# A linear-attention block with a routed feed-forward: the second attention product with swapped operands in four column tiles

## The reference, cut to what matters

```python
q, k, v = heads(x Wq + bq), heads(x Wk + bk), heads(x Wv + bv)     # b h s d
qp = relu(einsum('bhsd,hdf->bhsf', q, rw)) + EPS                   # EPS = 1e-6
kp = relu(einsum('bhsd,hdf->bhsf', k, rw)) + EPS
kv = einsum('bhsf,bhsd->bhfd', kp, v)
qkv = einsum('bhsf,bhfd->bhsd', qp, kv)
norm = einsum('bhsf,bhf->bhs', qp, kp.sum(axis=2))
x = layernorm(x + (qkv / (norm + EPS)) Wo + bo)
x = layernorm(x + ffn(x))     # gated mlp of width 1024, and experts chosen by product keys, 4 heads
```

## Time and profile before

| | |
|---|---|
| time, median of 3 runs | 3632.07 us (3629.95 to 3634.01) |
| profiled execution | 3635.19 us, span 3633.4 us |
| granted TensorE clock | 0.991 of full speed |
| instructions | 52250 |
| DMA | 61.17 MB, mean 17 GB/s |

### The profile page before, as it was taken

The page is one execution under the profiler, slowest core; times in us unless marked ns, Lnnn a source line. Parts: engine busy times, 40 slices in busy tenths (PEclk is TensorE's granted clock), DMA queues, the critical chain, the costliest instruction groups (busy, mean ns, idle before and its releaser), DMA issues.

```text
span 3633.4 us, 52250 instructions
## 1 busy us (share of the span) xinstructions
PE 3549.2 (98%) x19420; PEld 2929.1 (81%) x19420; DVE 2585.7 (71%) x5554; ACT 1981.3 (55%) x2886; POOL 1514.3 (42%) x1012
## 2 busy tenths in 40 slices
PE   8789999999999999999999999999999999999988
PEld 6668888888888888888888888888888888888877
DVE  4577777777777777777777777777677777777773
ACT  4455465555555555556555555555655554555551
POOL 0354344443344434444433444443444434555440
PEclk9899999999999999999999999999999999999999
DMA  3000000000000000000000000000000000000000
GB/s 118 18 12 18 13 13 12 18 18 12 12 18 12 18 18 13 12 18 13 18 18 13 13 13 18 18 14 17 13 12 18 18 7 12 13 13 12 7 6 12
DMA packets 23339, 61.17 MB, mean 17 GB/s; under 512 B 5552, under 2 KB 10032, under 8 KB 23088
## 3 DMA queue, kind: packets, MB, share of 16 engines
q1 hardware_dynamic: 18480, 41.04, 3.6%
q0 software_dynamic: 4608, 16.78, 1.1%
HBM read 41.04 MB, written 16.78 MB: 16 GB/s over the span
## 4 chain that ended last, share of the span: by engine, by line
PE 90%; DVE 3%; ACT 3%; POOL 1%; issue 1%; SPq 0%; DMA 0%; DVEq 0%; ACTq 0%; POOLq 0%
PE ring L639 28%; PE y_bank L732 12%; PE y_bank L734 11%; PE step_bank L554 6%; PE step_bank L562 6%; PE step_bank L666 6%; PE step_bank L639 5%; PE step_bank L598 3%; PE step_bank L656 3%; PE step_bank L548 3%; PE step_bank L590 3%; PE step_bank L712 3%; PE y_bank L728 1%; POOL grid L461 1%; DVE prob L1120 1%
## 5 line engine op out<-in xcount | busy, mean ns | idle before, releaser
L461 POOL TENSOR_TENSOR grid<-ex 128x1024 f32<-128x1024 f32 x512 | 1066.3, 2090 | 999.2 <-DVE prob L1117 364.3
L732 PE MATMUL y_bank<-wd_sb,gate 128*128 128x256 f32 x2048 | 621.6, 385 | 0.0
L734 PE MATMUL y_bank<-up_sb,wexp 128*128 128x256 f32 x2048 | 609.1, 379 | 0.0
L1107 DVE SCALAR_TENSOR_TENSOR grid<-grid,best 128x1024 f32<-128x1024 f32 x256 | 329.0, 1285 | 328.2 <-POOL grid L461 327.3
L1120 DVE SCALAR_TENSOR_TENSOR prob<-grid,narrow,prob 128x1024 f32<-128x1024 f32 x256 | 450.7, 1760 | 7.9
L639 PE MATMUL ring<-x1T_hl,downT_hl 128*128 128x512 f32 x1536 | 421.3, 409 | 17.2 <-ACT gate L883 17.2
L639 PE MATMUL ring<-x1T_hl,wg_hl 128*128 128x512 f32 x1536 | 428.8, 414 | 3.1 <-DVE gate L1136 3.1
L734 PEld LDWEIGHTS y_bank<-up_sb,wexp 128*128 128x128 f32 x2048 | 389.1, 190 | 52.8
L639 PE MATMUL ring<-x1T_hl,wu_hl 128*128 128x512 f32 x1536 | 422.2, 410 | 0.0
L732 PEld LDWEIGHTS y_bank<-wd_sb,gate 128*128 128x128 f32 x2048 | 354.0, 190 | 50.8 <-issue 22.7
L883 ACT ACTIVATE gate<-ring,bg_sb 128x512 f32<-128x512 f32 x256 | 176.3, 689 | 396.7 <-PE ring L639 395.0
(11 more groups left out here) (159 smaller groups left out, 5920.9 us busy)
## 6 DMA issues: line engine op xcount, KB each, us to landing
xb<-in_L_attn_x SPq DMA_DIRECT2D x34, 512.0 KB, 3.7
out_y<-x POOLq DMA_DIRECT2D x32, 512.0 KB, 3.0
xa<-in_L_attn_x SPq DMA_DIRECT2D x30, 512.0 KB, 3.7
prob<-in_L_ffn_down_embed SPq DMA_DIRECT2D x1, 1024.0 KB, 5.8
prob<-in_L_ffn_Wg SPq DMA_DIRECT2D x1, 1024.0 KB, 8.6
prob<-in_L_ffn_Wu SPq DMA_DIRECT2D x1, 1024.0 KB, 10.5
wd_sb<-in_L_ffn_Wd SPq DMA_DIRECT2D x1, 1024.0 KB, 11.4
up_sb<-in_L_ffn_up_embed SPq DMA_DIRECT2D x1, 1024.0 KB, 12.1
```

Source lines behind the costliest of these rows:

```text
L461: pool.tensor_tensor(grid[:, h % 2], bcast(ex[:, h, 0:NX].unsqueeze(2), [P, NX, NK]), bcast(ex[:, RH + h, 0:NK].unsqueeze(1), [P, NX, NK]) ...
L732: pe.matmul(rows, gate[:, c % 2, t * P:(t + 1) * P], wd_sb[:, c, :], start=(c == 0 and t % 2 == 0), stop=False, skip_group_check=True)
L734: mm = pe.matmul(rows, wexp[:, c % 2, t * P:(t + 1) * P], up_sb[:, c, :], start=False, stop=(c == C - 1), skip_group_check=True)
L1107: marks["keep", h] = rt_steps.mark(dve.scalar_tensor_tensor(out=g, in0=g, scalar=best[:, h, TOP - 1:TOP], in1=g, op0=ALU.is_ge, op1=ALU.mult))
```

## The change

The second product swaps its operands. The stationary operand is now 32 columns of `kv_blocks` (two heads by 16), the moving one qp with all 512 rows. Four such matmuls write the partitions 0, 32, 64 and 96 of one bank, so the result is transposed already, 128 of the 256 dimensions per bank. "num" gives the numerators so, and "den" the denominators, each repeated over its head's 16 dimensions, from a second set of blocks. The four "qkv" and two "back" uses become two "den" and two "num". ACT reads den, adding a constant, into `attnT` (now the memory of x1); DVE's new step "divide" takes the reciprocal of 128x512 in place and multiplies it with num plus a constant.

POOL no longer adds EPS to qp; a "consts" use after each fold multiplies the blocks with -0.5 and gives DVE the two constants. v is no longer biased: ACT copies it out of its bank, without bv. What bv adds is bv Wo, computed once into bo, less the EPS share in the constants. wo's sum and the norm's statistics are now in xb, and L1072's counterpart writes x1. xb's next load waits for that one. SP issues the store, in place of POOL. The uses stand at other chunks: den 0 and num 0 early in chunk 3, divide 0 in its middle, den 1 and num 1 early in chunk 5, divide 1 in its middle, wo 0 and wo 1 in chunk 6 as before.

In the tables qkv and back go; den and num get WORK 0.95 each and HOLD 2.0 and 8.0, consts 0.6 and 2.0. DVE's wait for y_stored moves to ACT's den 0; bv is loaded by element with the later weights.

```diff
@@ -59,10 +59,10 @@
               + [("v", 1)] + KV_TILE[2] + KV_TILE[3])
-    AT_SEQ = ([("turn", 0), ("turn", 1), ("q", 0), ("q", 1)] + [("qp", j) for j in range(4)] + [("qkv", 0)]
-              + [("qp", 4), ("qp", 5), ("qkv", 1), ("qp", 6), ("qp", 7), ("qkv", 2), ("qkv", 3)]
-              + [("back", 0), ("back", 1), ("wo", 0), ("wo", 1), ("next", 0), ("next", 1)])
-    KV_USES, AT_USES = len(KV_SEQ), len(AT_SEQ)
+    AT_SEQ = ([[("turn", 0)], [("turn", 1)], [("q", 0)], [("q", 1)]] + [[("qp", j)] for j in range(4)] + [[]]
+              + [[("den", 0), ("num", 0)], [("divide", 0), ("qp", 4)]] + [[("qp", j)] for j in range(5, 8)] + [[]]
+              + [[("den", 1), ("num", 1)], [("divide", 1)], [], [("wo", 0)], [("wo", 1)], []])
+    KV_USES = len(KV_SEQ)
     STEP_BANKS, FILL = 4, BG // 2
@@ -100,15 +101,16 @@
         kv_sum = sb("kv_sum", P, FC // 2 * P)
-        kv_blocks = sb("kv_blocks", P, FC, 2, DK + 1)
+        kv_blocks = sb("kv_blocks", P, 2, FC, 2, DK)
+        num_w, den_w = kv_blocks[:, 0], kv_blocks[:, 1]
...
         xbT = qp[:, 2:4]
-        den = sb("den", P, T, 4)
-        attnT = xbT
+        consts = sb("consts", P, 4)
         x1 = sb("x1", P, T, D)
+        attnT = x1[:].rearrange("p t d -> p (t d)").rearrange("p (h n) -> p h n", h=2)
         stats, mv1, rstd1 = sb("stats", P, T, 6), sb("mv1", P, T, 2), sb("rstd1", P, T)
@@ -177,20 +180,18 @@
-        AT_EARLY = [AT_SEQ[3 * c:3 * c + 1] for c in range(7)] + [[]]
-        AT_MID = [AT_SEQ[3 * c + 1:3 * c + 2] if c < 6 else [] for c in range(7)] + [[]]
-        AT_LATE = [AT_SEQ[3 * c + 2:3 * c + 3] for c in range(6)] + [[], AT_SEQ[-2:]]
-        AT_MID[6] = [("wo", 1)]
+        AT_EARLY, AT_MID, AT_LATE = ([AT_SEQ[3 * c + k] for c in range(C - 1)] for k in range(3))
+        AT_EARLY.append([]), AT_MID.append([]), AT_LATE.append([("next", 0), ("next", 1)])
         kv_places = [(c, place) for c in range(C) for place in range(3) if place or c >= C - 2]
...
-        WORK = {"turn": 0.44, "k": 1.73, "q": 1.73, "v": 1.73, "kp": 0.47, "qp": 0.46, "qkv": 1.73, "sum": 1.73,
-                "back": 0.44, "wo": 1.73, "next": 0.44, "rt": 1.39, "pt": 0.44, "fold": 2.6, "ff": 1.39, "out": 1.73}
-        HOLD = {"turn": 2.0, "k": 6.0, "q": 6.0, "v": 4.0, "kp": 2.0, "qp": 2.0, "qkv": 3.5, "sum": 3.0,
-                "back": 2.0, "wo": 3.0, "next": 5.0, "rt": 8.0, "pt": 5.0, "fold": 9.0}
+        WORK = {"turn": 0.44, "k": 1.73, "q": 1.73, "v": 1.73, "kp": 0.47, "qp": 0.46, "den": 0.95, "num": 0.95, "consts": 0.6, "sum": 1.73,
+                "wo": 1.73, "next": 0.44, "rt": 1.39, "pt": 0.44, "fold": 2.6, "ff": 1.39, "out": 1.73}
+        HOLD = {"turn": 2.0, "k": 6.0, "q": 6.0, "v": 4.0, "kp": 2.0, "qp": 2.0, "den": 2.0, "num": 8.0, "consts": 2.0, "sum": 3.0,
+                "wo": 3.0, "next": 5.0, "rt": 8.0, "pt": 5.0, "fold": 9.0}
         place, taken = {}, [0] * (STEP_BANKS + 2)
@@ -388,10 +390,14 @@
                     else:
-                        sp.wait_ge(*drained("at", m - 1, "wo", 1))
+                        sp.wait_ge(x1_ready, m * T)
                     sp.dma_start(xb[:], x_groups[m]).then_inc(xb_loaded, 16)
+                if last:
+                    sp.wait_ge(y_ready, (f + 1) * T)
+                    sp.dma_start(out_groups[f], y_sb[:]).then_inc(y_stored, 16)
             schedule(sp, body, lambda b: None)
+            sp.wait_ge(y_stored, 16 * NG)
@@ -440,13 +446,10 @@
                     pool.wait_ge(*full("at", m, "turn", 1))
+                    if m == 0:
+                        pool.wait_ge(bo_ready, 2)
                     pool.tensor_tensor(xb[:], xb[:], bcast(bo_sb[:].unsqueeze(1), [P, T, D]),
                                        ALU.add).then_inc(xb_bias, 1)
-
-                def qp_add(j):
-                    wait_apart(pool, drained("at", m, "qp", j))
-                    pool.tensor_scalar(qp[:, j % 4], qp[:, j % 4], ATTN_EPS, 1.0, ALU.add,
-                                       ALU.mult).then_inc(qp_eps, 1)
@@ -603,8 +594,29 @@
             pe.wait_ge(low_ready, 3)
+            for k in range(KD):
+                mm = pe.matmul(ring[0][:, 0:D], bv_sb[:, k:k + 1].broadcast_to([P, P]), wo_sb[:, k, :],
+                               start=(k == 0), stop=(k == KD - 1))
+            mm.then_inc(bo_full, 1)
             for k in (STEP_BANKS, STEP_BANKS + 1):
                 pe.wait_ge(bank_read[k], fill_taken[k])
+
+            def weights(kind, c):
+
+                return (num_w if kind == "num" else den_w)[:, c].rearrange("p g d -> p (g d)")
+
+            def consts_use(a):
+
+                bank = bank_of("kv", a, "consts", 0)
+                free(pe, "kv", a, "consts", 0)
+                pe.wait_ge(blocks_ready, 3 * (a // BG + 1))
+                pe.wait_ge(*drained("kv", a, "fold", 0))
+                for col, kind in enumerate(("num", "den")):
+                    for c in range(FC):
+                        row, at = 2 * DK * (c % 4), 2 * col + c // 4
+                        mm = pe.matmul(bank[row:row + 2 * DK, at:at + 1], weights(kind, c), neg_half[:, 0:1],
+                                       start=True, stop=True)
+                filled_by(mm, "kv", a, "consts", 0)
@@ -655,23 +669,19 @@
                                            qT_hl[:, j // 2, :], start=(part == 0), stop=(part == 1))
-                    elif kind == "qkv":
-                        pe.wait_ge(qp_eps, m * FC + 2 * j + 2)
-                        if j == 0:
-                            pe.wait_ge(blocks_ready, 3 * batch)
-                            pe.wait_ge(*drained("kv", batch * BG - 1, "fold", 0))
-                        W = 2 * (DK + 1)
-                        for t in range(T):
-                            for c in range(2):
-                                mm = pe.matmul(at_bank[:, (2 * t + c) * W:(2 * t + c + 1) * W],
-                                               qp[:, (2 * j + c) % 4, t * P:(t + 1) * P],
-                                               kv_blocks[:, 2 * j + c].rearrange("p a b -> p (a b)"),
-                                               start=True, stop=True)
-                    elif kind == "back":
-                        pe.wait_ge(*drained("at", m, "qkv", 2 * j + 1))
-                        mm = turn(at_bank, x1, j)
+                    elif kind in ("den", "num"):
+                        if kind == "den":
+                            for k in range(4):
+                                pe.wait_ge(*drained("at", m, "qp", 4 * j + k))
+                            if j == 0:
+                                pe.wait_ge(blocks_ready, 3 * batch)
+                                pe.wait_ge(*drained("kv", batch * BG - 1, "fold", 0))
+                        for k in range(4):
+                            mm = pe.matmul(at_bank[2 * DK * k:2 * DK * (k + 1), :], weights(kind, 4 * j + k),
+                                           qp[:, k, :], start=True, stop=True)
                     elif kind == "wo":
-                        pe.wait_ge(*drained("at", m, "back", 1))
+                        pe.wait_ge(*drained("at", m, "num", 0))
+                        pe.wait_ge(*drained("at", m, "num", 1))
                         mm = project_rows(at_bank, attnT, wo_sb, 2 * j)
@@ -848,8 +865,12 @@
                         read_by(act.activation(qp[:, j % 4, :], at_bank[:], ACT.Relu), "at", m, kind, j)
-                    elif kind == "back":
-                        read_by(act.copy(attnT[:, j, :], at_bank[:]), "at", m, kind, j)
+                    elif kind == "den":
+                        if last and j == 0:
+                            act.wait_ge(y_stored, (it - LAST_LAG + 1) * 16)
+                        act.wait_ge(*drained("kv", batch * BG - 1, "consts", 0))
+                        read_by(act.activation(attnT[:, j, :], at_bank[:], ACT.Identity,
+                                               bias=consts[:, 2 + j:3 + j]), "at", m, kind, j)
                     else:
@@ -998,23 +1015,35 @@
+            dve.wait_ge(w_loaded, W_ALL)
+            dve.tensor_scalar(bv_eps[:], bv_sb[:], -ATTN_EPS, None, ALU.mult).then_inc(bo_ready, 1)
+            dve.wait_ge(bo_full, 1)
+            dve.tensor_tensor(bo_sb[:], ring[0][:, 0:D], bo_sb[:], ALU.add).then_inc(bo_ready, 1)
+
             def blocks(b):
...
                 sums = bank[:, 0:FC * VW].rearrange("p (c w) -> p c w", c=FC)
-                bias = bv_sb[:].rearrange("p (c w) -> p c w", c=FC)
                 for g2 in range(2):
                     rows, cols = slice(g2 * F, (g2 + 1) * F), slice(g2 * DK, (g2 + 1) * DK)
-                    dve.scalar_tensor_tensor(out=kv_blocks[rows, :, g2, 0:DK], in0=bias[rows, :, cols],
-                                             scalar=ATTN_EPS * S, in1=sums[rows, :, cols], op0=ALU.mult,
-                                             op1=ALU.add).then_inc(blocks_ready, 1)
-                    ins = dve.tensor_scalar(kv_blocks[rows, :, g2, DK:DK + 1], sums[rows, :, 2 * DK:VW],
```

(40 more changed lines are left out.)

59 lines of the change are left out of this document (29 added, 30 removed).

## The result

The changed kernel takes 3730.83 us (median of 4 runs, 3728.46 to 3733.95) against 3632.39 (3629.95 to 3634.01): a ratio of 1.0272 (95% interval 1.0254 to 1.0290). It is 98 us slower. The forecast was 3553, range 3508 to 3620; it was wrong in sign. Its profiled execution took 3731.7 us against 3635.2 before, span 3729.9 against 3633.4; mean granted clock of TensorE 0.973 against 0.991.

The account below looks back on a forecast made before the run. TensorE, busy 98% of the span, was taken as the bound. 81 us from 26 groups plus 3 from 6 others, less 5 for consts and bv, gave 79: 3556 us profiled, 3553 median, range 3508 to 3620.

Parts of the forecast that it names:

- what TensorE loses and gets: TensorE per group: qkv and back going save 7.60 us, den and num cost 3.88, so 3.72 less, 119 over 32 groups.
- B: Rival for den and num: only two column tiles run at a time, 3628 us, no change; chance 0.07.
- C: Rival for den and num: tiles run one after another, 3848 us; chance 0.10 with what lies between it and B.
- the reciprocal: DVE's divide step: 3.35 us over 512 elements, bounds 0.7 and 8.1; a whole divide about 4.1 us.
- ACT's copies at nothing: ACT's copies of v and den against two copies back: 1.2 us more per iteration, with 47 to spare, priced at nothing.
- I take 0.6 us of waits per group: TensorE's waits for DVE's divides: 0.6 us per group, leaving 3.1 net, 81 us over 26 groups.
- kv_sum ... would end at +4.1 - 1.4: DVE in chunk 4: kv_sum ends at 2144.2, the kp needing a bank comes at 2144.5, 0 to 0.3 us to spare.
- POOL's L448: POOL's addition to qp going: 262.7 us of an engine not on the path, priced at nothing.
- rival D: DVE isn't felt: 3518 us profiled, 3515 median, 3508 if DVE gains from L448's absence; chance 0.70 together with the forecast.
- the consts use at 1 us: TensorE's 32 tiny passes once per batch: 1 us each, 4 for all batches, bounds 1 and 14.
- wo for DVE's multiplication, 0.4 to 1 us in about 30 cases: TensorE's first output projection waits for the divide in chunk 5: 0.4 us, up to 1.5 if ACT or POOL slips.
- Rival A: Divides give back most, each costing TensorE 1.2 to 1.6 us through late banks and wo: 3603 to 3621 us; chance 0.13.

Follow-up runs that it names:

- e6: The changed kernel with each divide directly behind den and num on DVE and consts' planned hold 14 us instead of 2: 3513.77 us, 0.9675.
- e9: e7 with den and num in two column tiles of 64 instead of four of 32, half the heads left out: 3603.97 us, 0.9919.
- e10: e7 with v copied out of its bank by DVE instead of ACT: 3503.97 us, 0.9643.
- e11: The changed kernel with v copied by DVE instead of ACT, that part undone alone: 3731.92 us, 1.0273.
- e7: e6 with DVE's additions apart in odd chunks, head 1 ahead of wexp, head 2 behind the key/value use: 3504.19 us, 0.9645.
- e4: The kernel before without POOL's addition of EPS to qp (L448), TensorE waiting for ACT's qp directly: 3641.05 us, 1.0025.
- e5: The changed kernel with each divide right behind den and num in DVE's order, ahead of h and keep 2: 3579.65 us, 0.9857.
- e1: The changed kernel with the reciprocal over 16 of 512 columns and den's ACT step scaled by 0, order kept: 3596.25 us, 0.9902.
- e2: The changed kernel with the planned hold of consts 14 us instead of 2, nothing else: 3664.31 us, 1.0085.

## Why the prediction was wrong

**Right: what TensorE loses and gets.** "Pair: 4 slots of 0.43 + 0.22 = 1.94 us with four tiles" measured 1.85, and e6 has the whole gain: 104.5 us against 108.9, 4.4 where 3.72 stood (the pairs account for 0.18 of the surplus; the rest isn't traced). Rivals B and C are out: two tiles measured 3.58 us a pair in e9. **Right too:** the reciprocal, 3.346 us against 3.35 from the slope of two short rows, and ACT's copies at nothing (e10, e11).

**Failed, and it decides: "I take 0.6 us of waits per group".** It rested on "kv_sum ... would end at +4.1 - 1.4", which left the kp in chunk 4 "tight, 0 to 0.3 us", and on qp 6 "also just in time". The waits measured 1.92 and 1.14 us, 26 and 20 times. TensorE came when forecast: 54.1 us into the iteration without the wait for qp 6 (2144.5 was 54.1). DVE didn't: kv_sum ended at 57.1 us where the forecast had 53.8. Two terms were missing in that sum. Keep 2 was to come 1.4 us sooner and came 0.3 later, because ACT's masks, taken as set by TensorE, were set by DVE, behind a long addition in its chunk 1 (e7 against e6, e4 against before). And the addition of head 2 between the divide and kv_sum, left at 1.28 us, takes 3.03 in every one of these chunks. The prediction saw 3.52 us of idle time ahead of keep 2 and took from it that DVE isn't late there; it is cover only for work that stands ahead of keep 2, and the divide stood behind it. e5 put the divide there, and the loss is gone with the same work.

**Failed: POOL's L448 "at nothing",** and in rival D even as a gain for DVE. Its absence makes DVE's addition the long one each time (e4). Where DVE isn't late that matters little: e4 lost 8 us, and e7 gained 10 on e6. In chunk 4 of the changed kernel it holds up kv_sum by 1.75 us directly and by about 1.1 through keep 2 (e7 against e6), together 2.9 of the 3.4 us by which kv_sum missed its forecast. By these figures, an estimate, the two waits there would have all but vanished without the crossing, divide and all; no run has the changed kernel with its additions apart and nothing else. So chunk 4 took both, the divide behind keep 2 and the long additions, and e1 and e5 take away the one.

**Failed: the consts use at 1 us.** The products take 0.38 us, less than taken. The "4 for all batches" is also a slip, since there are 8 of them; the 3 us measured came near it by luck. The sum priced the instruction and not the bank: its reader runs 15 us later, while the plan holds it for 2.0. Seven waits, 54.5 us, and the clock after them are 66.5 us by e2. When a bank's reader gets there was asked for num and not here.

**Failed: a wait priced at its own length.** No term stood for TensorE's clock. The row of 0.57, the doubled passes and the chunk of 14.59 us at full clock against 16.2 show it; over the span it is 67 us more than before, and e6, without the waits, is at 53 us of half clock, below the 70 of the kernel before.

**Half right: "wo for DVE's multiplication, 0.4 to 1 us in about 30 cases".** In the 26 full iterations it doesn't happen. It happens in the other six groups, for which the prediction did expect DVE to be felt but took 0.5 us of gain each: 4.0 us in each of the last four, 2.5 and 8.1 in the first two. The last four cost 30 us instead of giving 2; 7 of the 30 are the consts' wait (e2 has 103.7 in place of 110.7).

**Sum.** Against the forecast of the profiled execution (3556) 176 us are missing: 20 ordinary iterations at 3.9 (78), 6 batch ends at 11.2 (67), the last four 32. Rival A had the mechanism, a divide that makes banks late, but capped at "give back most"; it counted neither the long addition nor the clock. Its threshold, a reciprocal from 4.9 us on, is near the 3.35 + 1.75 that stood in the queue, but that is partly luck, since it knew neither the addition nor the clock. Rival D's 3518 for the profiled execution is a slip too: 3635 - 114 is 3521.

What stays open: why POOL's instruction ahead decides which engine pays for a crossing; what the changed kernel would take with only its additions apart; and why half clock followed the two waits of chunk 4 in all but one iteration here but in 16 of 20 in e2, whose chunk 4 took 14.6 us in the four others.

## What to carry to other kernels

Where a change moves work onto an engine with time to spare, ask at which place of its order the work stands and which banks' readers are queued behind it; idle time counts as cover only if the new work stands ahead of the wait that causes it. Give each new use of a shared bank the time until its reader in fact gets there: one wrong hold of 2.0 cost 66 us here. Price a wait of TensorE at more than its length (in chunk 4 3.0 us of waits cost 5.2), and try the order of the new steps before judging a change: the same 49408 instructions took 3731 and 3514 us.

## What the hardware showed

- Four column tiles of 32 for fp32 run at once: 16 passes of 512 columns in 1.85 us, against 3.58 in two tiles of 64; one after the other they would take 6.9, an estimate from the 0.43 of a pass by the earlier trace rows.
- Behind waits of 1.14 and 1.92 us, in an engine otherwise busy throughout, TensorE's granted clock was 0.57 over the next 3.4 us, in 19 of 20 iterations; chunk 4 took 16.2 us with it and 14.6 without. Half clock summed to 204 us in the changed kernel and 53 in e6.
- A DVE addition with two SBUF inputs took 3.03 us instead of 1.28 where a POOL tensor_tensor started within 0.05 us of it, or POOL's took 3.00 instead of 1.90; one of the two paid, never both. POOL paid where its instruction ahead was the addition to qp (62 of 62), DVE where it was another spread (66 of 66, and 128 of 128 without the addition to qp).
- A DVE reciprocal costs about 6.5 ns an element at 512 elements (3346 ns); from 16 elements (246 ns, e1) on each one adds 6.25 ns.
